# Leaving the gates unscaled in the row store: exponentials and an inverse sum in each gathered row, and a small product after the gather

## The reference: what is computed

```python
logits = x @ wg.T                                  # 64 experts
gates = jax.nn.softmax(logits, axis=-1)
w_topk, idx_topk = jax.lax.top_k(gates, TOPK)      # 8 of 64
w_topk = w_topk / w_topk.sum(-1, keepdims=True)
...                                                # tokens sorted by expert, at most 160 for each
out = jnp.einsum('ecf,ehf->ech', x1 * jax.nn.silu(x2), expert_w2)
y = out[se, rank] * sw[:, None]                    # the token's weight for that expert
combined = zeros.at[st].add(y)
return x + attention(xn) + (shared_out + combined)
```

## Time and profile before

| | |
|---|---|
| runs, us | 352.60, 352.67, 354.01 |
| profiled execution, us | 354.11 |
| its span, us | 352.30 |
| around the span, us | 1.81 |
| PE busy | 329.7 (94%) |
| POOL busy | 246.4 (70%) |
| DVE busy | 264.9 (75%) |
| ACT busy | 205.4 (58%) |
| TensorE clock over the span | 0.995 of full |

### The profile page before, as it was taken

The page is one execution under the profiler, slowest core; times in us unless marked ns, Lnnn a source line. Parts: engine busy times, 40 slices in busy tenths (PEclk is TensorE's granted clock), DMA queues, the critical chain, the costliest instruction groups (busy, mean ns, idle before and its releaser), DMA issues.

```text
span 352.3 us, 9275 instructions
## 1 busy us (share of the span) xinstructions
PE 329.7 (94%) x3067; PEld 309.2 (88%) x3067; DVE 264.9 (75%) x1076; ACT 205.4 (58%) x450; POOL 246.4 (70%) x251
## 2 busy tenths in 40 slices
PE   8999886999989999999999999999999999999994
PEld 7888775989989998999999889899999888999992
DVE  5898986887758677877878677878777866666685
ACT  5889716355646585647465946474767564764220
POOL 5977855466787678878786888688787787656600
PEclk9999999899999999999999999999999999999999
DMA  6999724599887878787878787878787768872598
GB/s 206 341 375 342 175 61 134 186 254 319 186 196 183 199 174 223 160 219 171 216 175 214 162 203 184 205 177 214 171 206 169 196 171 203 191 147 25 90 379 277
DMA packets 60110, 71.15 MB, mean 202 GB/s; under 512 B 14880, under 2 KB 47904, under 8 KB 60064
## 3 DMA queue, kind: packets, MB, share of 16 engines
q1 hardware_dynamic: 42592, 56.40, 51.9%
q0 software_dynamic: 15360, 13.12, 23.9%
q10 hardware_dynamic: 2112, 1.05, 1.0%
HBM read 54.72 MB, written 15.43 MB: 199 GB/s over the span
## 4 chain that ended last, share of the span: by engine, by line
PE 74%; ACT 7%; DVE 6%; DMA 6%; issue 5%; POOL 1%; SPq 1%; POOLq 0%; DVEq 0%; ACTq 0%
PE bank L1400 27%; PE bank L1410 12%; PE bank L1322 7%; PE bank L1333 4%; PE bank L1419 3%; PE bank L1447 3%; DMA ew<-acc 2%; PE bank L1487 2%; PE bank L1434 2%; ACT L574 2%; DMA ew<-in_expert_w 2%; PE bank L1479 2%; PE bank L1366 2%; PE bank L1453 1%; PE bank L1471 1%
## 5 line engine op out<-in xcount | busy, mean ns | idle before, releaser
L539 POOL DMA_INDIRECT acc<-ys,idx_g x64 | 105.0, 1641 | 38.9 <-issue 14.7
L1400 PE MATMUL bank<-xe,ew 128*128 128x160 f32 x768 | 117.2, 302 | 3.0 <-ACT xe L627 2.0
L1400 PEld LDWEIGHTS bank<-xe,ew 128*128 128x128 f32 x768 | 109.5, 191 | 5.7 <-ACT xe L627 2.3
L520 POOL DMA_INDIRECT gath<-xng,idx_g x80 | 81.2, 1014 | 32.2 <-issue 20.7
L602 ACT ACTIVATE si<-bank 128x480 f32<-128x480 f32 (+1 forms) x96 | 52.0, 542 | 61.7 <-PE bank L1400 23.9
L821 DVE TENSOR_TENSOR ac<-si,bank 128x480 f32<-128x480 f32 x64 | 41.7, 651 | 25.9 <-ACT si L602 19.8
L1410 PE MATMUL bank<-ew,ac 128*128 128x128 f32 x384 | 56.4, 283 | 1.3 <-issue 1.1
L1410 PEld LDWEIGHTS bank<-ew,ac 128*128 128x128 f32 x384 | 49.0, 193 | 3.0 <-issue 2.2
L1322 PE MATMUL bank<-xT,shw 128*128 128x128 f32 x384 | 50.5, 278 | 0.0
L1322 PEld LDWEIGHTS bank<-xT,shw 128*128 128x128 f32 x384 | 46.8, 192 | 0.5 <-ACT cum L727 0.2
L644 ACT ACTIVATE ys<-bank,gath 128x128 f32<-128x128 f32 x64 | 23.3, 364 | 22.5 <-PE bank L1410 15.7
(11 more groups left out here) (170 smaller groups left out, 570.2 us busy)
## 6 DMA issues: line engine op xcount, KB each, us to landing
ew<-in_expert_w SPq DMA_DIRECT2D x64, 384.0 KB
ew<-in_expert_w SPq DMA_DIRECT2D x64, 192.0 KB
ew<-acc SPq DMA_DIRECT2D x8, 512.0 KB, 7.1
xng<-xn SPq DMA_DIRECT2D x8, 256.0 KB, 5.4
acc<-zeros SPq DMA_DIRECT2D x4, 512.0 KB, 5.2
acc<-betas SPq DMA_DIRECT2D x4, 512.0 KB
x_sb<-in_x SPq DMA_DIRECT2D x7, 256.0 KB, 6.1
gath<-xng,idx_g POOLq DMA_INDIRECT x80
```

The costliest lines, as they stand in the source:

```text
L520: pool.indirect_dma_start(out=gath[:, p, m, :], out_offset=None, in_=xng, in_offset=bass.IndirectOffsetOnAxis(ap=idx_g[:, g % 5, m:m + 1], ...
L539: pool.indirect_dma_start(out=acc[adds_to[g, m]], out_offset=bass.IndirectOffsetOnAxis(ap=idx, axis=0), in_=src, in_offset=None, compute_o ...
L1400: last = pe.matmul(h_view(n, half_ + 1, CAP)[:, c, :], ew[p][m][:, k * P:(k + 1) * P], xe[:, p, m, :], start=True, stop=True)
```

## The change

A row of `xng` now has 193 numbers: `xn`, the 64 exponentials, and the inverse sum. `lg` gets a 65th column, into which DVE's reciprocal writes. POOL's four multiplications `gates(0)` to `gates(3)` are gone, and SP's stores wait for ACT's exponentials and DVE's reciprocal instead of POOL. After each group's rows are gathered, DVE multiplies the own exponential of each slot by its inverse sum, four numbers a partition (`slot_gates`), and ACT scales by this new tile `gate`; `rest_gate` takes a third factor. Three things move: `tile_bases` behind the two `offset`s on POOL, the `betas` copy on ACT from round 6 to between two `silu`s, and `first_counts(4)` on PE from round 6 to round 7.

```diff
-    ROW = D + E
+    ROW = D + E + 1
...
-        lg = sb("lg", [P, NT, E])
+        lg = sb("lg", [P, NT, E + 1])
+        gate = sb("gate", [P, 2, M])
...
             def gates_store(h):
-                sp.wait_ge(gw_ready, h + 1)
+                sp.wait_ge(ex_ready, h + 1 + (h == 3))
+                sp.wait_ge(wt_ready, h + 1)
...
-            def gates(h):
-                n = slice(*gated[h])
-                w = n.stop - n.start
-                pool.wait_ge(ex_ready, h + 1 + (h == 3))
-                pool.wait_ge(wt_ready, h + 1)
-                pool.tensor_tensor(lg[:, n, :], lg[:, n, :], wt[:, n].unsqueeze(2).to_broadcast([P, w, E]), ALU.mult).then_inc(gw_ready, 1)
...
             less_max(2)
-            gates(0)
             less_max(3)
-            gates(1)
             less_max(4)
-            gates(2)
-            gates(3)
-            tile_bases()
             offset(0)
             offset(1)
+            tile_bases()
...
-                act.activation(ys[:, m, :], Y[:, 0:P], ACT.Copy,
-                               scale=gath[:, g % 2, m, D + M * g + m:D + M * g + m + 1]).then_inc(y_done, 1)
+                act.wait_ge(gate_done, g + 1)
+                act.activation(ys[:, m, :], Y[:, 0:P], ACT.Copy, scale=gate[:, g % 2, m:m + 1]).then_inc(y_done, 1)
...
                 if r == 6:
-                    act.wait_ge(s_vec, 16)
-                    act.activation(betas[:, :].rearrange("p (k d) -> p k d", d=D), beta_b.unsqueeze(1).to_broadcast([P, 8, D]), ACT.Copy).then_inc(betas_set, 1)
                     exps(2)
...
             silu(('s', 5))
+            act.wait_ge(s_vec, 16)
+            act.activation(betas[:, :].rearrange("p (k d) -> p k d", d=D), beta_b.unsqueeze(1).to_broadcast([P, 8, D]), ACT.Copy).then_inc(betas_set, 1)
             silu(('s', 6))
...
-                dve.reciprocal(wt[:, n], tsum[:, n]).then_inc(wt_ready, 1)
+                dve.reciprocal(lg[:, n, E], tsum[:, n]).then_inc(wt_ready, 1)
...
-                dve.tensor_tensor(wr_t[:, :], gath[:, g % 2, M, D + M * g:D + M * g + M], block4[:, :], ALU.mult).then_inc(wr_step, 1)
+                dve.scalar_tensor_tensor(wr_t[:, :], gath[:, g % 2, M, D + M * g:D + M * g + M], gath[:, g % 2, M, D + E:ROW], block4[:, :],
+                                         ALU.mult, ALU.mult).then_inc(wr_step, 1)
...
+            def slot_gates(g):
+
+                for m in range(M):
+                    dve.wait_ge(g_in[g % 2][m], 16 * (g // 2) + 16)
+                if g > 1:
+                    dve.wait_ge(y_done, down_at['e', g - 2, 3] + 1)
+                rows_ = gath[:, g % 2, 0:M, :]
+                own_ = rows_.rearrange("p m r -> p (m r)")[:, D + M * g:D + M * g + (M - 1) * (ROW + 1) + 1:ROW + 1]
+                dve.tensor_tensor(gate[:, g % 2, :], own_, rows_[:, :, D + E], ALU.mult).then_inc(gate_done, 1)
...
                 expert_mul(g, 0)
+                if g > 0:
+                    slot_gates(g)
...
                     expert_mul(g, 1)
+                    slot_gates(g)
...
                     first_counts(3)
+                if r == 7:
                     first_counts(4)
-                if r == 7:
                     first_counts(5)
```

More of the change, by code:

```diff
@@ L150, in block_kernel @@
         mask = sb("mask", [P, NT + 1, E], bf16)
-        tsum, wt = sb("tsum", [P, NT]), sb("wt", [P, NT])
+        tsum = sb("tsum", [P, NT])
         cum = sb("cum", [E, 4, RB, P], fp16)
@@ L222, in block_kernel @@
         top_ready, left_ready, mask_ready = sem("top_ready"), sem("left_ready"), sem("mask_ready")
-        topm_ready, lgm_ready, etop_ready, ex_ready, tsum_ready, wt_ready, gw_ready = (sem(n) for n in
-            ("topm_ready", "logits_less_max", "exp_top_ready", "exp_ready", "tsum_ready", "wt_ready", "gw_ready"))
+        topm_ready, lgm_ready, etop_ready, ex_ready, tsum_ready, wt_ready, gate_done = (sem(n) for n in
+            ("topm_ready", "logits_less_max", "exp_top_ready", "exp_ready", "tsum_ready", "wt_ready", "gates_of_slots"))
         diag_ready, bounds_done, within_full, cum0_done, qk0_full, qk0_done = (sem(n) for n in
@@ L441, in less_max @@
                 pool.tensor_tensor(topm[:, n, :], top[:, n, :], top[:, n, 0:1].to_broadcast([P, w, TOPK]), ALU.subtract).then_inc(topm_ready, 1)
[L442 removed]
+                pool.tensor_tensor(lg[:, n, 0:E], lg[:, n, 0:E], top[:, n, 0:1].to_broadcast([P, w, E]), ALU.subtract).then_inc(lgm_ready, 1)
             def tile_bases():
@@ L589, in logits_copy @@
                 act.wait_ge(q_full, q_at['logits', r] + 1)
-                act.activation(lg[:, tiles(r), :].rearrange("p j e -> p (j e)"), AQ[:, 0:RB * E], ACT.Copy).then_inc(q_done, 1)
+                act.activation(lg[:, tiles(r), 0:E], AQ[:, 0:RB * E].rearrange("p (j e) -> p j e", e=E), ACT.Copy).then_inc(q_done, 1)
             def cum_copy(r):
@@ L608, in exps @@
                 act.wait_ge(lgm_ready, k + 1)
-                act.activation(lg[:, n, :], lg[:, n, :], ACT.Exp).then_inc(ex_ready, 1)
+                act.activation(lg[:, n, 0:E], lg[:, n, 0:E], ACT.Exp).then_inc(ex_ready, 1)
             def narrow_copy(q):
@@ L841, in largest @@
                 for t in range(RB * r, RB * r + RB):
-                    dve.max(top[:, t, :], lg[:, t, :]).then_inc(top_ready, 1)
+                    dve.max(top[:, t, :], lg[:, t, 0:E]).then_inc(top_ready, 1)
             def chosen(r):
@@ L847, in chosen @@
                 for j in range(RB):
-                    dve.match_replace(left[:, j, :], top[:, RB * r + j, :], lg[:, RB * r + j, :], LOW).then_inc(left_ready, 1)
+                    dve.match_replace(left[:, j, :], top[:, RB * r + j, :], lg[:, RB * r + j, 0:E], LOW).then_inc(left_ready, 1)
                 dve.wait_ge(left_ready, RB * (r + 1))
```

## The result

The changed kernel takes 362.24 us in the median of 4 runs (360.81 to 364.87), the kernel before 353.22 (4 runs, 352.60 to 354.01). The ratio is 1.027, with a 95% interval of 1.021 to 1.032: the medians differ by 9.0 us. Forecast were 352.3 us, in a range of 350.9 to 353.9. All ratios in this text are taken from the fast executions alone, so they can differ by up to 0.3% from the quotient of the medians given beside them.

A forecast was written before the change was run, and what follows sets the result against it. PE was taken to bound the kernel, with 74% of the chain. Only the 0.35 us from `oh` before `table(0)` counted, all else zero: 352.67 - 0.35 = 352.3 us, range 350.9 to 353.9.

The forecast's parts named there:

- Rows of 193 numbers ... By size alone, nothing: DMA of `xng` rows: 260 bytes stored instead of 256, 772 gathered instead of 768; 0.5% by size, no time.
- crooked rows: Rival, chance 0.05: gathers of rows starting off 256 bytes take 0.2 us more each, four make 0.8; 353.1 us.
- DVE's `oh`: DVE's row of hots before PE's `table(0)`: without POOL's products beside it, 0.5 to 0.6 us; gain 0.35 us.
- The offsets: POOL's two instructions of 0.947 us each, expected from 39.4 to 41.3, still busy when `oh` starts at 40.93.
- Stores earlier, nothing gained: SP's gate stores: the last can go about 1.8 us earlier, but row numbers come later than its landing; zero gain.
- the gate stores were late after all: Rival, chance 0.11: the first gather waited for the gates' landing, so 0.65 us more goes; 351.7 us.
- `betas`, `first_counts(4)`: Moves on ACT and PE: 1.05 us hidden in ACT's idle time, 8 matmuls in PE's; zero gained.
- `slot_gates`: DVE, between `expert_mul` and `u`: 2.8 us hidden in idle time, so zero; rival that it shows, 355.4, chance 0.07.
- The three-factor `rest_gate`: DVE's product in each group, widened from two to three factors: expected to stay at 0.17 us.
- The low clock: PE's 1.2 GHz stretch: hold or low clock gone, 350.8, chance 0.10; low clock typical, 353.7, chance 0.08.

The follow-up runs named there:

- b_rows193: The kernel before with only the row lengthened to 193 numbers by a zero 65th column, POOL's products kept: 348.28 us against 339.63, ratio 1.025.
- before_again: The kernel before, unchanged, traced again on the chip of three of the versions in one profiled execution: 338.87 us.
- 288/800: The changed kernel with stored pieces padded to 288 bytes and rows to 800 bytes, measured twice: ratios 1.001 and 0.999.
- 272/784: The changed kernel with stored pieces of 272 bytes and rows of 784 bytes: 344.13 us against 339.75, ratio 1.011.
- b_moves: The kernel before with only the moves of `betas`, `first_counts(4)` and the offsets, POOL's products kept: 355.61 us against 353.19, ratio 1.009.
- a_wide72: The changed kernel with rows padded to 200 numbers and stored pieces to 72, the padding zero: first measurement, ratio 1.001.
- a_counts_act: The changed kernel with the last store of the counts issued on ACT's own queue instead of SP's: 363.67 us against 353.19, ratio 1.028.

## Why the prediction was wrong

**The step that failed** is "Rows of 193 numbers ... By size alone, nothing", and with it the rival "crooked rows". That rival had the right cause, and the right sign, at the wrong place and a tenth of the size: it priced the gathers, 0.2 us each and 0.8 in all, and gave itself 0.05. The gathers cost next to nothing: their median landing is 3.6 us in b_rows193 and 3.9 in before_again (where the trace has it, 8 and 40 of the 80), and their packets of six rows take 301 ns against 298 there, 305 against 283 in the changed kernel and the one before. The stores cost it, 4096 pieces of 260 bytes at 46 ns instead of 18. The working had the store's landing in hand, "by 42.09 + 2.5 = 44.6", but took the 2.5 us from pieces of the old shape, as if a DMA of the same size had the same duration. With 8.5 it would have read 50.6, five microseconds behind the row numbers; the last store itself landed at 51.27.

The Trainium skill, on the page DMA: Bandwidth & Descriptors, section How a descriptor splits into AXI transactions, prices a start off 256 bytes by added beats of reading. By its count (an estimate: 25 to 32 beats of 32 bytes for 772 bytes, 24 for 768) a gathered row would cost a fifth more in the mean and a third at most; the packets above took 1% and 8% more. Rows at 800 or 832 bytes mostly start off 256 and cost nothing here that the time shows, so that rule doesn't order these versions. Another does, though it stands in the Trainium skill for the buffers of collectives: on the page Collectives: The Full Stack, section Rules for kernel authors, a buffer is to be 32-byte aligned, as this "Prevents HW read-modify-write". The table fits it: 288/800 at 1.001 and 0.999, 272/784 at 1.011. That a read-modify-write is the mechanism no run here shows.

**DVE's `oh`**: right, and cautious. 0.38 us instead of the 0.5 to 0.6 forecast. Counted from DVE's `top` of 22.83 us, `table(0)` comes 20.55 us later; before it was 21.12, counted from 21.95. The gain is the full 0.57 us. The offsets, priced at 0.947 us each from rows that were themselves slowed by DVE, took 0.7 each. So they were over at 41.6, ahead of `oh`. That POOL's two-input products and DVE's hold each other is also what b_moves shows; the Trainium skill's page SBUF — State Buffer, section SBUF: two separate sides, calls it an exclusive lock, and 0.57 us added to `oh` in the four traces with the products and none in the ten without agrees with it.

**Stores earlier, nothing gained**: nothing was gained, but not for the reason given. Even the aligned pieces land after 3.9 us instead of 2.5, and their landing, not the row numbers, now sets the first gather: in a_wide72 the last store lands at 45.24 and the gather starts at 46.33, 0.35 us later than the numbers alone (45.05 + 0.93) would let it. Counted from `table(0)` the aligned versions gather 0.4 to 0.9 us later than before. No loss can be measured from it. The rival "the gate stores were late after all" was wrong: in the kernel before the last landed at 44.23, and a gather 1.09 us behind it would have started at 45.3, ahead of 46.21.

**`betas`, `first_counts(4)`**: hidden, as said. From `top` of round 3 to `oh` it is 18.98 us before, 18.99 in b_moves and 18.98 after. `betas` took 1.06 us at 43.85.

**`slot_gates`**: hidden, as said. The groups of the changed kernel by line and shape:

```profile
L937 DVE SCALAR_TENSOR_TENSOR wr_t<-gath,cpack 128x4 f32<-128x4 f32 x16 | 3.6, 224 | 0.0
L952 DVE TENSOR_TENSOR gate<-gath 128x4 f32<-128x4 f32 x16 | 2.5, 157 | 0.0
```
```profile
L993 DVE TENSOR_TENSOR u<-bank,bqk 128x512 f32<-128x512 f32 x16 | 11.0, 689 | 7.3 <-PE bank L1452 6.5 <-issue 0.7
```

16 products of 157 ns make 2.5 us, and the idle time before `u` fell from 9.4 to 7.3. The three-factor `rest_gate` takes 0.224 us, not the 0.17 expected, 0.8 us more in all, hidden too. The working has three groups without idle time before `u`; in the trace before, it is five of the 16 (the longest of them 0.04 us). It made no difference.

**The low clock**: it was named as the open end of both signs, with 1.4 us at stake. In the changed kernel it stands for up to 4.4 us of the 10.7 that the trace loses, but the loss doesn't need it: b_rows193 loses as much with no low clock between its first expert and group 1. The forecast treated it as a coin toss; by the runs it comes with PE's idle time, if not in step with it: the seven versions whose first gather starts after 49 us have 3.4 to 17.0 us of it before 80 us, the four of them in which PE waits over 4 us for the counts at least 6.8. Of the seven executions that start earlier, three have none and four have 3.4 to 6.8.

## What to carry to other kernels

Before a row or piece in HBM gets one more number, look at where its pieces then begin and end: a store of many small pieces is priced by their edges before it is priced by its bytes. Padding 260 bytes to 288 took back 2.5% of this kernel at no cost that could be measured. When a step changes a transfer's shape, don't take its duration from the old shape; bound it from above, and ask who waits for this landing and what PE's idle time then does to its clock. And price an order together with what stands ahead of it: the moves cost 0.9% by themselves and nothing that can be measured once the products were gone.

## What the runs showed of the hardware that was not expected

- Pieces of 260 bytes with both ends off 32 bytes: 46 to 50 ns a packet in the mean, single ones up to 1519, against 17.9 and 19 for 256 bytes and 22.7 and 91 for 288. One crooked end: 28 to 29 ns.
- They slow other stores beside them too. The 64 packets of 1024 bytes of the counts' last store, which are aligned themselves, take 46.0 ns in the mean before, 111 after (one 1036), 159 in b_rows193 and 128 by ACT's queue in a_counts_act; beside aligned pieces of 288 bytes it is 74, beside 512 bytes 46.
- When POOL's and DVE's products of two inputs meet, the one that comes second is held. In the kernel before, `ohm` starts at 42.13, ahead of POOL's offsets at 42.22: `ohm` keeps its 0.68 us, and the two offsets take 1.86 instead of 1.41. In b_moves the offsets run when `ohr` and `ohm` come, and these take 0.70 and 1.21 us instead of 0.29 and 0.68.
- The same kernel before has a median of 353.2 us in two of the comparisons and of 339.6 and 339.8 in two others, on other chips. The ratios carry over: 1.027 beside the slower one, 1.025 (b_rows193) beside the faster, for the same fault.
- The start of a profiled execution varies: DVE's `top` of round 3 begins at 21.95 to 23.06 us in the 14 traces, ahead of the lines that were changed. A place in the trace is compared by its distance from an earlier mark, not by its time.
